# Causal attention kernel: the diagonal is masked on the exponentials, not on the scores

## The reference

```python
scores = jnp.einsum('bthd,bshd->bhts', q, k)
mask = jnp.tril(jnp.ones((T, T), dtype=scores.dtype))
scores = scores * mask
attn = jax.nn.softmax(scores / T ** 0.5, axis=-1)
out = jnp.einsum('bhts,bshd->bthd', attn, v)
```

## Time and profile before

| | us |
|---|---|
| median of 3 runs | 1850.01 |
| lowest and highest | 1845.79, 1854.95 |
| span of the profiled execution, first to last instruction | 1842.1 |
| PE, POOL, DVE, ACT busy in it | 1707.1, 779.7, 1103.2, 734.6 |

### The profile page before, as it was taken

The page is one execution under the profiler, slowest core; times in us unless marked ns, Lnnn a source line. Parts: engine busy times, 40 slices in busy tenths (PEclk is TensorE's granted clock), DMA queues, the critical chain, the costliest instruction groups (busy, mean ns, idle before and its releaser), DMA issues.

```text
span 1842.1 us, 29048 instructions
## 1 busy us (share of the span) xinstructions
PE 1707.1 (93%) x9634; PEld 974.0 (53%) x9634; DVE 1103.2 (60%) x1792; ACT 734.6 (40%) x957; POOL 779.7 (42%) x452
## 2 busy tenths in 40 slices
PE   4899999994989999999999998999999999989977
PEld 4777788773644444444444444444444444433655
DVE  7655566635966756665775664666577566310567
ACT  3223333220034445444455444544445544556311
POOL 0000000003026556555555554555555655477641
PEclk9999999995569999999999999999999999989988
DMA  5555555449620054036016005403502600221698
GB/s 171 155 177 174 169 183 178 154 166 215 139 54 7 7 116 110 7 70 152 7 39 162 32 7 123 106 7 70 151 7 52 169 12 7 85 78 30 194 339 300
DMA packets 109499, 201.78 MB, mean 110 GB/s; under 512 B 13856, under 2 KB 31776, under 8 KB 108320
## 3 DMA queue, kind: packets, MB, share of 16 engines
q1 hardware_dynamic: 98256, 177.79, 35.3%
q10 hardware_dynamic: 11088, 22.02, 3.6%
HBM read 123.22 MB, written 76.28 MB: 108 GB/s over the span
## 4 chain that ended last, share of the span: by engine, by line
PE 70%; DVE 8%; issue 8%; POOL 5%; DMA 5%; ACT 2%; SPq 1%; ACTq 0%; POOLq 0%; DVEq 0%
PE psM L1104 16%; PE psS L1130 13%; PE psO L1152 13%; PE psP L1051 9%; DVE mx L908 6%; PE psP L1064 5%; PE psL L1160 5%; POOL acc L645 4%; DMA gr<-gate 3%; PE psP L1075 3%; PE psS L1133 2%; PE psM L1107 2%; PE psL L1168 2%; PE psT L1006 2%; ACT Pb L739 1%
## 5 line engine op out<-in xcount | busy, mean ns | idle before, releaser
L908 DVE TENSOR_REDUCE mx<-psM 128x1 f32<-128x512 f32 (+3 forms) x1028 | 666.2, 673 | 355.7 <-PE psM L1104 183.2
L645 POOL TENSOR_TENSOR acc<-acc,Pb 128x1024 f32<-128x1024 f32 (+2 forms) x320 | 615.2, 1939 | 433.2 <-ACT Pb L739 340.2
L739 ACT ACTIVATE Pb<-psS 128x1024 f32<-128x1024 f32 (+3 forms) x576 | 485.2, 880 | 503.9 <-PE psS L1130 267.7
L1104 PE MATMUL psM<-Ks,Qs 96*128 96x512 f32 (+3 forms) x1174 | 457.5, 436 | 34.2 <-DMA Ks<-k_lo 22.1
L1130 PE MATMUL psS<-Qs,Ks 97*128 97x512 f32 (+3 forms) x1280 | 441.6, 411 | 31.7 <-ACT Pb L739 17.2
L1104 PEld LDWEIGHTS psM<-Ks,Qs 96*128 96x128 f32 x1174 | 221.0, 198 | 344.8 <-DVE mx L908 287.8
L1130 PEld LDWEIGHTS psS<-Qs,Ks 97*128 97x128 f32 x1280 | 244.0, 198 | 122.0 <-ACT Pb L739 55.9
L1152 PE MATMUL psO<-Pb,Vs 128*32 128x512 f32 (+3 forms) x2304 | 267.6, 536 | 0.0
L590 POOL TENSOR_TENSOR rstd<-ve,mhalf 128x4 f32<-128x4 f32 x16 | 16.2, 1010 | 321.8 <-DVE ve L818 321.8
L1160 PE MATMUL psL<-Pb,ones 128*32 128x512 f32 (+1 forms) x1024 | 122.1, 549 | 0.0
L1133 PE MATMUL psS<-negt,identb 128*128 128x128 bf16 x512 | 117.3, 237 | 0.0
(11 more groups left out here) (109 smaller groups left out, 1726.8 us busy)
## 6 DMA issues: line engine op xcount, KB each, us to landing
Qs<-q_hi SPq DMA_DIRECT2D x32, 512.0 KB, 12.9
Ks<-k_hi SPq DMA_DIRECT2D x32, 512.0 KB, 10.8
xt<-in_L_attn_x SPq DMA_DIRECT2D x8, 1024.0 KB, 6.1
q_hi<-st_hi SPq DMA_DIRECT2D x32, 256.0 KB, 3.2
q_lo<-st_lo SPq DMA_DIRECT2D x32, 256.0 KB, 3.3
k_hi<-st_hi SPq DMA_DIRECT2D x32, 256.0 KB, 4.0
k_lo<-st_lo SPq DMA_DIRECT2D x32, 256.0 KB, 4.3
v_quad<-vs SPq DMA_DIRECT2D x32, 256.0 KB, 3.3
```

What stands on the lines that cost most here:

```text
L645: g.tensor_tensor(acc[c % 2][p][:, :, o:], acc[c % 2][p][:, :, o:], Pb[ring(s)][p][:, :, o:], ALU.add).then_inc(sum_done, 1)
L739: a.activation(W[p][:, :, o:], psS[p][:, :, o:], ACT.Exp, scale=SCALE).then_inc(exp_done, 1)
L908: v.tensor_reduce(flat[:, first:first + step * (ns - 1) + 1:step], banks[k % len(banks)][:, 0:ns * w].rearrange("p (a b) -> p a b", a=ns), ...
L1104: ins = t.matmul(bank[:, at:at + w], Q[0:STACK, h, tile * P:(tile + 1) * P], K[0:STACK, h, k0:k0 + w], start=True, stop=not diag)
```

## The change

On the diagonal the scores are no longer masked. GpSimd instead writes zeros above the diagonal into the exponentials, with one affine select per pair and diagonal step, on the 128 columns of each of the two heads, in place. Each select waits for the exponential of its pair and raises a new semaphore, `sel_done`. On diagonal steps the values matmul and the sum in `acc` wait for that semaphore. `negt` and its two setup instructions are gone. In GpSimd's order the selects of a step stand before everything else of that step.

```diff
+def on_diagonal(s):
+    c, j = STEPS[s]
+    return j >= CT * c
+
+def diagonals_before(s):
+    return sum(on_diagonal(i) for i in range(s))
+
+NDIAG = diagonals_before(NSTEP)
...
-            g.memset(negt[:], 0.0).then_inc(const_c, 1)
+            g.memset(Ks[0][MROW:MROW + 1, :, :].bitcast(F32), 1.0).then_inc(const_c, 1)
             pool.wait_ge(const_c, 8)
-            g.affine_select(out=negt[:], in_=negt[:], compare_op=ALU.is_ge, fill=-BIG, base=0,
-                            pattern=[[1, P]], channel_multiplier=-1).then_inc(const_c, 1)
...
             def quad(qn, par, more, load):
                 for s, (c, j) in enumerate(STEPS):
                     o = max(0, j - CT * c) * P
                     step = qn * NSTEP + s
+                    if on_diagonal(s):
+                        W = acc[c % 2] if j == 0 else Pb[ring(s)]
+                        for p in range(NPAIR):
+                            pool.wait_ge(exp_done, START + step * NPAIR + p + 1).then_inc(pool_waited, 1)
+                            tile = W[p][:, :, o:o + P]
+                            g.affine_select(out=tile, in_=tile, compare_op=ALU.is_ge, fill=0.0, base=0,
+                                            pattern=[[0, 2], [1, P]], channel_multiplier=-1).then_inc(sel_done, 1)
...
                         for p in range(NPAIR):
-                            pool.wait_ge(exp_done, START + step * NPAIR + p + 1)
+                            if on_diagonal(s):
+                                pool.wait_ge(sel_done, (qn * NDIAG + diagonals_before(s)) * NPAIR + p + 1)
+                            else:
+                                pool.wait_ge(exp_done, START + step * NPAIR + p + 1)
...
-                                       Q[0:MROW + 1, h, c * CW + o:(c + 1) * CW], start=True, stop=j < CT * c)
-                        if j >= CT * c:
-                            ins = t.matmul(psS[p][:, e, o:o + P], identb[:], negt[:], start=False, stop=True)
+                                       Q[0:MROW + 1, h, c * CW + o:(c + 1) * CW], start=True, stop=True)
...
                         if h % 2 == 0:
-                            pe.wait_ge(exp_done, START + step * NPAIR + p + 1)
+                            if on_diagonal(s):
+                                pe.wait_ge(sel_done, (qn * NDIAG + diagonals_before(s)) * NPAIR + p + 1)
+                            else:
+                                pe.wait_ge(exp_done, START + step * NPAIR + p + 1)
```

More of the change, by code:

```diff
@@ L215, in build @@
         negm = sbuf(pc, "negm", [P, P], BF16)
-        negt = sbuf(pc, "negt", [P, P], BF16)
         zrow = sbuf(pc, "zrow", [P, HQ, NT], F32)
@@ L290, in build @@
         const_c = sem("const_c")
-        FOR_MAXIMA, FOR_SCORES = 7, 11
+        FOR_MAXIMA, FOR_SCORES = 7, 9
         kq_low = [sem(f"kq_low{i}") for i in range(2)]
@@ L310, in build @@
         sum_done = sem("sum_done")
+        sel_done = sem("sel_done")
         L_full = sem("L_full")
@@ L611, in _ @@
             pool.wait_ge(const_c, FOR_MAXIMA)
-            g.memset(negt[:], 0.0).then_inc(const_c, 1)
+            g.memset(Ks[0][MROW:MROW + 1, :, :].bitcast(F32), 1.0).then_inc(const_c, 1)
             pool.wait_ge(const_c, 8)
-            g.affine_select(out=negt[:], in_=negt[:], compare_op=ALU.is_ge, fill=-BIG, base=0,
-                            pattern=[[1, P]], channel_multiplier=-1).then_inc(const_c, 1)
-            pool.wait_ge(const_c, 9)
-            g.memset(Ks[0][MROW:MROW + 1, :, :].bitcast(F32), 1.0).then_inc(const_c, 1)
-            pool.wait_ge(const_c, 10)
             g.memset(Ks[1][MROW:MROW + 1, :, :].bitcast(F32), 1.0).then_inc(const_c, 1)
@@ L622, in _ @@
                    allow_small_or_imprecise_dtypes=True).then_inc(const_c, 1)
-            pool.wait_ge(const_c, 12)
+            pool.wait_ge(const_c, 10)
             def quad(qn, par, more, load):
```

## The result

The changed kernel takes 1874.0 us (median of 4 runs, 1866.9 to 1876.4) against 1852.5 for the kernel before on the same chip: ratio 1.0115, 95% interval 1.0087 to 1.0143. It is slower by 21.5 us, where 20.9 was forecast. A later series of runs gave 1.0143 (1.0122 to 1.0164), 25 us by its medians.

The account below looks back on a forecast made before the run. TensorE's instruction stream was taken to bound seven quads and GpSimd's sums the last. Waits of 25.6 + 5.7 - 23.8 = +7.5 us plus 13.4 for the clock made +20.9 on 1850.0, rounded to 1870; range 1849 to 1892.

Parts of the forecast that it names:

- chunk 3, seven quads: Chunk 3 of the seven quads: the gain from the removed masks pays for the four selects, net 0.
- The masks: Chunks 1 and 2 of seven quads: 32 removed mask matmuls of 0.107 us save 3.4 us a quad, 23.8 in all.
- The select: Each added GpSimd select of 128x256 f32 takes 0.45 us, bounds 0.31 and 0.73.
- Rival C: Selects on GpSimd take 0.73 us each, adding 18 us, 1889 with the clock drops; chance 0.18.
- The wait in chunk 0: Chunk 0 of every quad: values of step 2 wait for selects behind GpSimd's sum, 3.2 us a quad, 25.6 over eight.
- Chunks 1 and 2 hidden: Chunks 1 and 2 of seven quads: selects finish before the values of r = 2 need them, about 0.3 us left.
- The last quad: Chunks 1 to 3 of the last quad: later GpSimd sums cost +1.0, +2.35 and +2.35, together 5.7 us.
- The waits together: Whole kernel: 25.6 + 5.7 - 23.8 = +7.5 us, before any drop of the clock.
- The clock: After chunk 0's gap TensorE's clock halves, costing 3.35 us a drop, 0 to 27 us; half taken, 13.4 us.
- A: Only the wait in chunk 0, no drop of the clock: 1857.5 us; chance 0.22.
- B: A mask matmul costs TensorE its full 237 ns, so chunks 1 and 2 save 53 us: 1828; chance 0.10.
- D: The wait of chunk 0 doesn't show, as TensorE's maxima are done in another wait's gap: 1832 us; chance 0.05.

Follow-up runs that it names:

- the first experiment: The changed kernel with its selects and the waits for them switched off, so neither masks nor selects: 1825.5 us, 0.9885 of the kernel before.
- the third: The changed kernel with chunk 0 masked by matmuls as before and chunks 1 to 3 by selects: 1837.7 us, 0.9950 of the kernel before.
- the kernel with the changed order: The changed kernel with GpSimd's instructions of chunk 0 reordered, selects of steps 1 and 2 ahead of the sum of step 1: 1860.1 us, 1.0060 of the kernel before.

## Why the prediction was right

**Direction, size and place.** The forecast was 1870 with a wait in chunk 0 and a fall of the clock behind it; both are shown, by masks in chunk 0 (the place) and by idle matmuls (the clock apart from the wait). That 21.5 us came so close to 20.9 is in part luck, because errors of the sum cancel; the second series has 25 us. The kernel with idle matmuls has the waits without most of the falls of the clock, and its trace against the one before shows the parts (us):

| term | forecast | measured |
|---|---|---|
| chunk 0, eight quads | +25.6 | +25.1 |
| chunks 1 and 2, seven quads | -23.8 | -16.7 |
| chunk 3, seven quads | 0 | -3.0 |
| chunks 1 to 3, last quad | +5.7 | +1.8 |
| sum of the waits | +7.5 | +7.2 |

**The masks: 0.12 us each, 23.8 us in all.** Near in price (1.55 us for the 16 masks of chunk 1, 0.097 each, where the sum has 0.107) and too large in sum by 7 us. Without masks and selects the kernel gained 21 us, but part of it in places where I had nothing. Chunk 2 gave half of its 1.7, probably because VectorE's maxima became the wait there, which the prediction did not look for. Chunk 3 ended 0.7 earlier where its clock held; with the next chunk 0 counted in, that is 0.2, near the 0 I had. The masks of the last quad were worth 2.4 us (106.0 against 108.4), not nothing.

**The select: 0.45 us.** 408 ns as the mean. Rival C, 0.73 us, is out.

**The wait in chunk 0: 3.2 us a quad.** 3.9 with the clock held, 3.1 with the earlier end of chunk 3 set against it. The steps are as predicted: the products later by 1.9 us (2.05 less 0.18; predicted 1.58 from a start 0.24 earlier, 1.82), then the sum, then the selects of step 2. The gap was put at 3.4 us and is 3.95. (The 993.41 of the working should be 993.37 by its own terms, 992.92 + 0.45; nothing hangs on it.)

**Chunks 1 and 2 hidden, with 0.3 us to spare.** Right, and narrow: 0.2 us before the values of r = 2 in chunk 1, and doubling the selects costs 1.8 and 1.35 us a chunk.

**The last quad: +5.7 us for chunks 1 to 3.** Too large: +3.2, of which chunks 2 and 3 gave 2.95 and 2.3 (predicted 2.35 each), while chunk 1 got faster by 2.1 instead of slower by 1.0. In the kernel before the clock was down in that chunk; the windows of chunk 1 in quad 7, before and after, show 0.73 and 0.88:

```profile
1608.33:1637.80 29.47, 26.42 (x145) 11.06 (x145) 8.25 (x6) 14.41 (x19) 18.98 (x10) 0.73 0.30 103
```

```profile
1637.62:1665.03 27.41, 21.02 (x128) 8.25 (x128) 9.13 (x5) 14.00 (x19) 22.75 (x18) 0.88 0.26 92
```

I had counted a fall of the clock in the kernel before as normal work. Against the kernel with neither masks nor selects the last quad is 5.6 us longer, as the 5.7 say; what I left out are the 2.4 us of its masks. How much of the difference in chunk 1 is masks and how much clock wasn't tried: in the other traces that chunk takes 29.0 to 29.9 us with masks and 27.6 to 28.7 without.

**The waits together, +7.5.** With idle matmuls in the gap the kernel is at 1.0017, +3 us (-1 to +7), and +7.2 by the last marks of the traces.

**The clock: 13.4 us, half of the quads.** This term was too small. Quads 1 to 7 all have a granted clock of 0.65 to 0.82 in chunk 0, and the falls cost 18 to 23 us by the ratios. Two steps of the working made it small. Both gaps of over 3 us that I had read were followed by a fall, so nothing in the rows spoke for half of the quads. And the 6.7 us came from one of the two; behind the other, of 3.05 us, the same trace shows 0.50 for 12.8 us:

```profile
1628.19:1641.00 12.81, 12.81 (x64) 6.66 (x68) 0.69 (x1) 6.49 (x9) 5.00 (x4) 0.50 0.06 20
```

Why a fall lasts 4 us in one place and 14 in another wasn't tried. In the medians the small term is made up for by waits that are smaller in sum than +7.5 (+3) and by the changed kernel's other executions, which are 0.3, 4.4 and 9.5 us under the profiled one. Between the two traces, 32.5 us against 20.9, it is not made up for.

Of the rivals, A (the wait alone) is what the kernel with idle matmuls shows: 1851, not what the change does. B falls with the first experiment and D with the third.

## What to carry to other kernels

Moving work off the busiest engine onto a less busy one helps only if nobody waits for it behind something else in that engine's order: here the selects took 0.41 us each and the sum ahead of them 3.75. Count a gap on TensorE twice, for the wait and for the slow clock after it, which here cost as much as all masks together gained (18 to 23 us against 21); a gap can be filled with useless matmuls (which here only brought the time back to that of the kernel before), or the moved work left out in the few places where it opens one (0.9908). Look also for who becomes the wait when the gain comes: half of it in chunk 2 was lost, probably to VectorE.

## What the hardware did that was not expected

- After a gap of 3.97 us TensorE stayed at a granted clock of 0.50 for 14.3 us of uninterrupted work in quad 1 of the changed kernel, and after one of 3.96 us for some 4 us in quad 3. In the kernel before it was 6.7 us after 3.68 and 12.8 after 3.05.
- At the end of a quad the granted clock fell (to 0.75 over 6 us) in three of seven quads once the mask matmuls of chunk 3 were gone, with no idle stretch over 0.97 us; with them it fell in none of 21.
- A gap of 2.02 us brought the clock down in quad 3 of the kernel with the changed order and didn't in quad 5, with the same matmuls ahead of it and a clock of 1.00 in both. The length of a gap alone didn't decide. In the last quad of the kernel before, a gap of 2.01 us (up to 1606.32) was followed by 0.50 too, from 1608 to 1612.
- Adding 3.46 us of matmuls whose output nobody reads made each quad faster by 2 to 3 us on average.
- GpSimd's in-place select of 128x256 f32 takes 408 ns where its two-tensor sum of the same size takes 731.
